# Cross-attention on one core: V crosses DRAM as fp32 and is split per batch, and the row maximum moves to the end of its slot

## The reference

```python
a = _layer_norm(audio_kv, ln_gamma, ln_beta)
Q = (hidden_states @ Wq.T).reshape(B, Tt, HEADS, HEAD_DIM).transpose(0, 2, 1, 3)
K = (a @ Wk.T).reshape(B, Ta, HEADS, HEAD_DIM).transpose(0, 2, 1, 3)
V = (a @ Wv.T).reshape(B, Ta, HEADS, HEAD_DIM).transpose(0, 2, 1, 3)
scores = jnp.einsum('bhtd,bhsd->bhts', Q, K) * scale        # scale = 64 ** -0.5
scores = jnp.where(mask, scores, jnp.float32(-jnp.inf))
attn = jax.nn.softmax(scores, axis=-1)
out = jnp.einsum('bhts,bhsd->bhtd', attn, V)
out = out.transpose(0, 2, 1, 3).reshape(B, Tt, D) @ Wo.T
return hidden_states + jnp.tanh(gate) * out                 # (8, 1024, 1024)
```

## Time and profile before

| | us |
|---|---|
| median of three runs | 1492.25 |
| profiled execution | 1494.74 |
| its span in the profile | 1493.0 |
| PE busy | 1467.3 (98%) |
| VectorE busy | 1163.7 (78%) |
| ScalarE busy | 894.1 (60%) |
| GpSimd busy | 537.7 (36%) |
| granted clock of TensorE, mean | 1.0 |

### The profile page before, as it was taken

One profiled execution on the slowest core, in us unless ns is written; L12 is line 12 of the kernel. 1 busy time (PEld: TensorE's weight loads), 2 busy tenths in 40 slices (PEclk: granted clock), 3 DMA queues, 4 the chain that ended last, 5 costly groups with the idle time before them and its releaser, 6 DMA issues.

```text
span 1493.0 us, 20136 instructions
## 1 busy us (share of the span) xinstructions
PE 1467.3 (98%) x6624; PEld 1194.6 (80%) x6624; DVE 1163.7 (78%) x1349; ACT 894.1 (60%) x1894; POOL 537.7 (36%) x364
## 2 busy tenths in 40 slices
PE   6999999999999999999999999999999999999999
PEld 5666788888888888888787788888888888888887
DVE  6445788787878787979866788888888888888843
ACT  4556655455555555555776667766777776677521
POOL 5334000000000000000124566677766667776640
PEclk9999999999999999999999999999999999999999
DMA  7699865657575747474579988788887878888732
GB/s 281 215 376 391 292 216 198 216 199 231 183 233 174 242 159 257 142 253 132 168 254 328 297 250 243 235 248 244 265 267 238 234 242 248 242 265 266 212 118 84
DMA packets 303144, 348.51 MB, mean 233 GB/s; under 512 B 35648, under 2 KB 177088, under 8 KB 303040
## 3 DMA queue, kind: packets, MB, share of 16 engines
q1 hardware_dynamic: 287808, 332.54, 70.2%
q10 hardware_dynamic: 15232, 14.68, 2.8%
HBM read 198.26 MB, written 145.75 MB: 230 GB/s over the span
## 4 chain that ended last, share of the span: by engine, by line
PE 89%; DVE 3%; DMA 3%; issue 1%; SPq 1%; ACT 1%; POOL 1%; DVEq 0%; ACTq 0%; POOLq 0%
PE banks L1194 29%; PE banks L1196 29%; PE banks L1195 29%; PE banks L1223 3%; DMA m_scratch<-m_stage 1%; DMA probs<-s_scratch 1%; DVE parts L983 1%; DMA b_raw<-m_stage 1%; DVE a_ring L977 1%; PE banks L1262 0%; SPq L475 0%; DVE b_raw L1003 0%; DMA b_raw<-m_scratch 0%; PE banks L1188 0%; DVE a_sum L1047 0%
## 5 line engine op out<-in xcount | busy, mean ns | idle before, releaser
L1194 PE MATMUL banks<-parts,a_ring 128*128 128x512 f32 x1792 | 699.5, 390 | 4.3 <-DVE a_ring L977 3.5
L1196 PE MATMUL banks<-parts,a_ring 128*128 128x512 f32 x1792 | 697.5, 389 | 0.0
L1195 PE MATMUL banks<-parts,a_ring 128*128 128x512 f32 x1792 | 697.2, 389 | 0.0
L1194 PEld LDWEIGHTS banks<-parts,a_ring 128*128 128x128 f32 x1792 | 336.4, 188 | 76.2 <-DVE a_ring L977 6.1
L1196 PEld LDWEIGHTS banks<-parts,a_ring 128*128 128x128 f32 x1792 | 336.3, 188 | 70.2
L1195 PEld LDWEIGHTS banks<-parts,a_ring 128*128 128x128 f32 x1792 | 336.4, 188 | 69.3
L977 DVE TENSOR_TENSOR a_ring<-a_sum,a_ring 128x1024 fp32r<-128x1024 f32 x128 | 227.1, 1774 | 76.6 <-ACT a_ring L748 76.5
L748 ACT CAST a_ring<-a_sum 128x1024 fp32r<-128x1024 f32 x128 | 134.3, 1049 | 233.8 <-PE banks L1196 205.3
L1072 DVE TENSOR_TENSOR c_out<-banks,c_out 128x1024 f32<-128x1024 f32 x158 | 192.0, 1215 | 100.4 <-PE banks L1196 98.6
L818 ACT ACTIVATE probs<-probs,neg_max 128x64 f32<-128x64 f32 x1024 | 258.6, 337 | 1.2 <-DVE neg_max L1086 1.2
L657 POOL TENSOR_TENSOR probs<-probs,row_rec 128x512 f32<-128x512 f32 x128 | 134.6, 1052 | 241.3 <-DVE row_rec L1095 241.3
(11 more groups left out here) (77 smaller groups left out, 1350.8 us busy)
## 6 DMA issues: line engine op xcount, KB each, us to landing
xq<-x_t SPq DMA_DIRECT2D x32, 1024.0 KB, 6.2
s_scratch<-c_out SPq DMA_DIRECT2D x64, 512.0 KB, 3.1
probs<-s_scratch SPq DMA_DIRECT2D x128, 256.0 KB, 4.2
c_out<-x SPq DMA_DIRECT2D x63, 512.0 KB, 5.5
out<-c_out SPq DMA_DIRECT2D x63, 512.0 KB, 4.2
b_raw<-m_scratch SPq DMA_DIRECT2D x29, 1024.0 KB, 6.8
m_scratch<-m_stage SPq DMA_DIRECT2D x16, 1792.0 KB, 14.0
p_scratch<-p_turned SPq DMA_DIRECT2D x448, 64.0 KB, 2.6
```

Source lines behind the costliest of these rows:

```text
L1194: pe.matmul(to, wl, mh, start=first, stop=False, skip_group_check=joined)
L1195: pe.matmul(to, wh, ml, start=False, stop=False, skip_group_check=joined)
L1196: return pe.matmul(to, wh, mh, start=False, stop=last, skip_group_check=joined)
```

## The change

V is no longer split before it is stored: ScalarE copies each scaled tile as fp32 (`copy_v`), VectorE's eight low parts of V fall away, `v_scratch` and `v_out` have half the size, and V's second half of products waits for the copies instead of the low parts. `load_v` brings fp32 values into the place of the low part (`v_raw` lies on `v_diag`). Three slots before a group of four pairs is first used, ScalarE rounds two blocks of 64 partitions x 4 x 64 into the high part (`split_v_hi`) and VectorE subtracts it from the values in place (`split_v_lo`): 16 groups, two of each instruction in a group. PE waits for these low parts instead of the load. Besides, VectorE's row maximum moves behind the low part and the turned blocks of its slot.

```diff
-    v_scr = nc.dram_tensor("v_scratch", [B * S, NC, 2, P], F32, kind="Internal").ap()
+    v_scr = nc.dram_tensor("v_scratch", [B * S, D], F32, kind="Internal").ap()
...
+        v_raw = at("v_raw", 120, [P, NC, 2, P])
...
-        v_out = [at("v_out0", 32, [P, CT, HC, 2, P], F32R), at("v_out1", 96, [P, CT, HC, 2, P], F32R)]
+        v_out = [at("v_out0", 32, [P, CT, HD]), at("v_out1", 96, [P, CT, HD])]
...
+        def v_split(z):
+
+            return [(b, four) for b in range(B) for four in range(2) if values_at(16 * b + 4 * four) // 4 - 3 == z]
...
             def store_v(half):
-                sp.wait_ge(v_lo_made, CT * (half + 1))
-                to = v_scr[:, HC * half:HC * (half + 1)].rearrange("(i p) g t e -> p i (g t e)", p=P)
-                sp.dma_start(to, v_out[half][:].rearrange("p i g t e -> p i (g t e)").bitcast(F32)
+                sp.wait_ge(v_made, CT * (half + 1))
+                sp.dma_start(v_scr[:, HD * half:HD * (half + 1)].rearrange("(i p) e -> p i e", p=P), v_out[half][:]
                              ).then_inc(v_stored[half], 16)
...
-                    src = v_scr[b * S:(b + 1) * S, 4 * four:4 * four + 4, :, rr].rearrange("s g t e -> s (g t) e")
-                    to = v_diag[rr, 4 * four:4 * four + 4, :, rr].rearrange("s g t e -> s (g t) e")
-                    sp.dma_start(to.bitcast(F32), src).then_inc(v_in[four], 16)
+                    src = v_scr[b * S:(b + 1) * S, HD * four:HD * (four + 1)].rearrange("s (g e) -> s g e", g=4)
+                    sp.dma_start(v_raw[rr, 4 * four:4 * four + 4, 1, rr], src[:, :, rr]).then_inc(v_in[four], 16)
...
-            def copy_v_hi(half, i):
+            def copy_v(half, i):
                 act.wait_ge(v_done, CT * half + i + 1)
...
-                nc.scalar.activation(v_out[half][:, i, :, 0, :], banks[:, 4 + i, :].rearrange("p (g e) -> p g e", g=HC), ACT.Copy,
-                                     scale=v_scale[:, i:i + 1]).then_inc(v_hi_made, 1)
+                nc.scalar.activation(v_out[half][:, i, :], banks[:, 4 + i, :], ACT.Copy, scale=v_scale[:, i:i + 1]
+                                     ).then_inc(v_made, 1)
...
+            def split_v_hi(b, four):
+                act.wait_ge(v_in[four], 32 * (b + 1))
+                for h in range(2):
+                    rr = slice(h * HEAD, (h + 1) * HEAD)
+                    nc.scalar.copy(v_diag[rr, 4 * four:4 * four + 4, 0, rr], v_raw[rr, 4 * four:4 * four + 4, 1, rr]
+                                   ).then_inc(v_hi_made, 1)
...
                     for u in units(soft_slot, z - EXP):
                         exponential(u)
+                    for b, four in v_split(z):
+                        split_v_hi(b, four)
...
-            def split_v_lo(half, i):
-                dve.wait_ge(v_hi_made, CT * half + i + 1)
-                nc.vector.scalar_tensor_tensor(out=v_out[half][:, i, :, 1, :],
...
+            def split_v_lo(b, four):
+                dve.wait_ge(v_hi_made, 4 * b + 2 * four + 2)
+                for h in range(2):
+                    rr = slice(h * HEAD, (h + 1) * HEAD)
+                    hi, lo = (v_diag[rr, 4 * four:4 * four + 4, t, rr] for t in range(2))
+                    nc.vector.tensor_tensor(lo, v_raw[rr, 4 * four:4 * four + 4, 1, rr], hi.bitcast(F32), ALU.subtract
+                                            ).then_inc(v_lo_made, 1)
...
-            for i in range(2):
-                split_v_lo(1, i)
             for s in range(STEPS):
...
-                if s == 0:
-                    for i in range(2, CT):
-                        split_v_lo(1, i)
...
                     for u in units(soft_slot, z - SUM):
                         sum_rows(u)
-                    for u in units(soft_slot, z - MAX):
-                        row_max(u)
                     for u in units(split_slot, z):
                         if u < ON_PE:
                             split_p_lo(u)
                     for u in units(soft_slot, z - TURN):
                         if u >= ON_PE:
                             turn_blocks(u)
+                    for u in units(soft_slot, z - MAX):
+                        row_max(u)
+                    for b, four in v_split(z):
+                        split_v_lo(b, four)
...
-                        pe.wait_ge(v_lo_made, i + 1)
+                        pe.wait_ge(v_made, i + 1)
...
-                    pe.wait_ge(v_in[j // 4], 32 * (m // 2 + 1))
+                    pe.wait_ge(v_lo_made, 2 * m + 2 * (j // 4) + 2)
...
-                        pe.wait_ge(v_lo_made, CT + 2)
+                        pe.wait_ge(v_made, CT + 2)
```

More of the change, by code:

```diff
@@ L155, in xattn_kernel @@
         v_done = sem("v_done")
-        v_hi_made = sem("v_hi_made")
-        v_lo_made = sem("v_lo_made")
+        v_made = sem("v_made")
         v_stored = sems("v_stored", 2)
@@ L177, in xattn_kernel @@
         v_in = sems("v_in", 2)
+        v_hi_made = sem("v_hi_made")
+        v_lo_made = sem("v_lo_made")
         s_in = sems("s_in", PROBS)
@@ L853, in _ @@
                     for i in range(CT):
-                        copy_v_hi(0, i)
+                        copy_v(0, i)
             for q in range(2, 4):
@@ L862, in _ @@
             for i in range(CT):
-                copy_v_hi(1, i)
+                copy_v(1, i)
             for s in range(STEPS):
@@ L965, in copy_m @@
                                       ).then_inc(m_copied_b, 1)
-            def split_v_lo(half, i):
-                dve.wait_ge(v_hi_made, CT * half + i + 1)
-                nc.vector.scalar_tensor_tensor(out=v_out[half][:, i, :, 1, :],
-                                               in0=banks[:, 4 + i, :].rearrange("p (g e) -> p g e", g=HC),
-                                               scalar=v_scale[:, i:i + 1], in1=v_out[half][:, i, :, 0, :].bitcast(F32),
-                                               op0=ALU.mult, op1=ALU.subtract).then_inc(v_lo_made, 1)
             def split_a_lo(s):
@@ L1121, in _ @@
                     split_k_lo(half)
-                elif c == NC - 1 and half == 0:
-                    for i in range(CT):
-                        split_v_lo(0, i)
             for q in range(2, 4):
```

## The result

The changed kernel takes 1509.68 us (median of four runs, 1508.11 to 1512.18) against 1493.65 (1492.04 to 1496.14) for the kernel before, now over four runs: ratio 1.0107, 95% interval 1.0085 to 1.0130. The forecast was 1494.0 with a range of 1487.2 to 1499, so it was wrong. The profiled execution took 1509.14 us, with a span of 1507.4, 14.4 us more than the profiled one of before.

The account below looks back on a forecast made before the run. Only PE's idle microseconds could be won, and new waits outlasting its queue lost: -1.5 - 1.6 - 1.3 + 0.1 + 6.0 = +1.7 on the profiled 1494.74 us, 1496.4, or 1494.0 on the median's scale; range 1487.2 to 1499.

Parts of the forecast that it names:

- The opening: Start of main loop: V's halved store starts step 0 earlier, -1.5 us; low parts off VectorE remove later waits, -1.6 us.
- Rival C: Opening doesn't gain: M's landings don't move or ScalarE's copies hold step 1; 1495.5 to 1497.1 us, chance 0.13.
- The row maximum: Turn from score to output rounds: moving it removes PE waits at 805.21 and 819.05, part returned behind SyncE; -1.3 us.
- The first pair near 730 us: First two V differences, in the turn, ahead of the first low part of the probabilities: +0.1 us.
- V's two loads on SyncE: In the turn, SyncE's issue of V's loads, 1.28 us, gets some 0.4 us shorter with half the rows.
- They run back to back to 1115.55: Before step 163, both V differences run unparted after GpSimd's sum; step 1.0 us late, six times, +6.0 us.
- the race with GpSimd's sum: Before step 163, V's differences, ready about 1112.7, lose to GpSimd's sum begun at 1112.54, held off until 1114.93.
- rival B: Output rounds: GpSimd's p_parts parts the two differences, 2.15 us a time, 12.9 in all; 1500.9 us, chance 0.12.
- Rival A: Output-round stalls don't come, as casts are ready before GpSimd's sum begins; 1487.9 us, chance 0.25.

Follow-up runs that it names:

- e7: Changed kernel with each half of V also stored to a spare scratch ahead of the store that counts: 1510.82 us, ratio 1.0117 to the kernel before.
- e1: Kernel before with only the row maximum moved behind the low part and the turned blocks: 1492.45 us against 1493.41, ratio 0.9993.
- e2: Changed kernel with the row maximum back in its old place: 1510.51 us, ratio 1.0110 to the kernel before.
- e8: Changed kernel with one early cast and one difference a group, row maximum in its old place: 1491.5 us against 1493.67 for the kernel before, ratio 0.9984.
- e5: Changed kernel with ScalarE's casts of V at the head of their slot, ahead of output copies and exponentials: 1492.23 us, ratio 0.9994 to the kernel before.
- e3: Changed kernel with one cast and one difference over 128 partitions a group instead of two each: 1495.25 us against 1493.24 for the kernel before, ratio 1.0013.
- e9: Changed kernel with one cast over all partitions and the difference cut in two by columns: 1507.37 us, ratio 1.0097 to the kernel before.
- e6: Changed kernel with one cast and one difference over all partitions, the cast at the start of its slot: 1489.22 us, ratio 0.9974 to the kernel before.

## Why the prediction was wrong

**The opening was right.** Forecast -1.5 for the start of step 0 and -1.6 for steps 1 to 5; measured -1.53 and -1.73. e7 gives back the first with the bytes and little of the second, as the two terms said. Rival C is out.

**The row maximum came out by itself, in part by luck.** Forecast -1.3 for the turn: -0.6 at 805.21, -1.8 at 819.05, and a part given back behind SyncE's fetch. The maximum alone (e1) gives -1.23 in one trace, with -0.50, -1.99 and +2.34 at these three places. But steps 104, 119 and 121, which the sum did not have, moved by -0.59, +0.79 and -1.55, and the medians differ by 0.96 us, with an interval that takes in no change. The -1.8 was also not the maximum's own: with V's split it goes without the move (e2, e8).

**The first pair near 730 us was mis-sized.** Forecast +0.1, "but the maximum has left from there"; measured +1.04 at step 104 (also +1.01 in e5 and +1.03 in e7), where the maximum alone gave -0.59 (e1). The term priced only the pair's 0.6 us on a free VectorE, while GpSimd's normalisation began 0.16 us behind it and parted it. Another small term was off as well: V's two loads on SyncE, put 0.4 us shorter, take 1.27 us (1.28 before). The rest of the turn can't be told piece by piece: the changed kernel and e7, with the same order there, have turns of 145.67 and 143.48 us in one profile each.

**The step that failed is the one in the output round: "They run back to back to 1115.55".** The prediction saw the race with GpSimd's sum, its loser and the margin (0.1 to 0.2 us forecast, 0.3 in the trace), and queued the output sum and the factor behind the pair as they came. But it let the two differences run together, on the strength of five VectorE instructions that kept GpSimd out. They parted, in all six rounds, and the step started 2.24 us late instead of 1.0. That is rival B, priced at 2.15 us a time; it was given 0.12 and left out of the range. Where two instructions become one the forecast's 1.0 us appears, measured at 0.95 (e3), so the queue behind the pair was summed rightly. The rule that the prediction quoted from the Trainium skill, SBUF — State Buffer, section "Who interferes with whom", that issue order decides, was set against one row of the opening and lost; here it holds, with the waiting p_parts between the halves of a pair (3.83 us) and of e9's (4.03).

That row of the opening was also read too narrowly. GpSimd's instruction ends at 27.36, 1.48 us after the five differences (25.88). A GpSimd instruction of this shape that VectorE has held off ends some 1.15 us after it is let in: 1116.02 to 1117.16 in the earlier trace rows, 1116.84 to 1118.01 in the changed kernel. By that estimate it was let in at 26.21, which is the end of the next VectorE instruction, one with a single tensor operand:

```profile
25.80 0.41 DVE L933 TENSOR_SCALAR mask_f<-mask_u 128x512 f32<-128x512 uint8 x1
```

So what kept GpSimd out there was not, or not only, that the five were differences in a row, and the row was weak evidence for a pair of another kind.

**What no case held is the clock.** Rival B's 12.9 us for six stalls became 17.5: 0.5 from their size, 3.5 in the two steps with a fall of the granted clock and 0.6 in the four others, whose first products start further apart. With the turn (+0.67 instead of -1.2) this carries the time beyond B's 1500.9. The prediction priced a stall at its length; one of 2.1 us also risks 1.6 more behind it.

**Rival A** did not come about for the reason that was given against it, casts that are ready after GpSimd's sum has begun: e5 moves them alone and the stalls are gone, at 616.08 us for the output rounds.

So the change had a gain of 3.3 us in the opening, a part in the turn that runs from 0.8 us lost (e5, where the first pair is parted) to 2.9 us gained (e6, where it is one instruction), each in one trace, and a loss of 17.5 us that hung on where two casts of 0.8 us stood and, with them late, on the difference being two instructions. With both mended (e6) it is 0.26% faster than before.

## What to carry to other kernels

Before adding a VectorE instruction with two SBUF operands, read what GpSimd has running and queued at that microsecond: the price is the wait for both, not the instruction's own time, and it falls on all that is queued behind. Make such work one instruction rather than two, even over twice the partitions, with inputs early enough to run before GpSimd's long one. And price a stall of TensorE with the clock that may fall behind it.

## What the hardware showed that was not expected

- A pair of VectorE instructions of 0.3 us each took 3.83 us beside GpSimd: GpSimd's queued instruction got in after the first. In the opening GpSimd began at 24.21, between the third of five differences and the fourth, and was kept out by those that followed. What makes the difference was not settled. It is not that GpSimd there had been idle and began within the row: at 726.75 it did so too, after 4.53 us of idle time and 0.16 us into the pair, and got in after the first difference (0.37 us; the second took 1.16). The partition halves are ruled out as well (e9). Left untried are the size (512 elements there, 256 here) and the number in a row.
- After 2.08 us without TensorE work the granted clock fell to 0.50 and was back at 1.00 within 5 us (1121 to 1126), at a cost of 1.6 us; it did so at two of six equal stalls in the changed kernel, three of six in e2 and the one at 730 us there, two in e7 and one in e9 (1.94 to 2.27 us of idle time), and at none of e3's stalls (0.77 to 0.79 us) or of the waits in the turns, up to 1.81 us in the kernel before. What picks the stalls was not tried.
